# A written-out program with skewed half scans for a convolution, attention and state-space block

## The reference, cut to what matters

```python
x = x + L0(_gn(x))     # group norm, then linear attention with a depthwise 5x5 convolution
x = x + L1(_gn(x))     # group norm, layer norm, then a selective scan (Mamba)

# inside L0: q, k = elu + 1; key weights by a softmax over tokens; rotary turn; kv = k^T v
res = (q_rope @ kv) * z + depthwise5x5(v)
out = w_proj @ (res * o) + b_proj

# inside L1, for each of 4 channel groups of 32 (64 inner channels, 16 states):
def step(h, inp):
    u_t, d_t, B_t, C_t = inp
    h = exp(d_t[:, :, None] * A) * h + (d_t * u_t)[:, :, None] * B_t[:, None, :]
    y = einsum('nds,ns->nd', h, C_t)
    return h, y
# y * silu(z) -> W_out -> skip -> layer norm -> projection
```

## Time and profile before

| | |
|---|---|
| runs of the kernel before | 363.38, 365.04, 365.83 us; median 365.04 |
| profiled execution | span 364.0 us; its own time is not listed apart, the median lies 1.0 above the span |
| VectorE busy | 272.0 us, 75% |
| TensorE busy (matmul) | 273.2 us, 75% |
| ScalarE busy | 218.2 us, 60% |
| GpSimd busy | 201.7 us, 55% |
| transfers | 61.73 MB, 52.6% of the 16 DMA engines' time |

### The profile page before, as it was taken

One profiled execution on the slowest core, in us unless ns is written; L12 is line 12 of the kernel. 1 busy time (PEld: TensorE's weight loads), 2 busy tenths in 40 slices (PEclk: granted clock), 3 DMA queues, 4 the chain that ended last, 5 costly groups with the idle time before them and its releaser, 6 DMA issues.

```text
span 364.0 us, 5551 instructions
## 1 busy us (share of the span) xinstructions
PE 273.2 (75%) x1882; PEld 130.7 (36%) x1882; DVE 272.0 (75%) x334; ACT 218.2 (60%) x408; POOL 201.7 (55%) x135
## 2 busy tenths in 40 slices
PE   1596894899594866987998669878966776965763
PEld 1264552344232333533453235325522211421321
DVE  1632156999212599787999897979999988999992
ACT  2334777563843798359775985697667637552211
POOL 0030302576250279827875797377758666876760
PEclk9999898569788799898799999988999756585598
DMA  7230409730159907782689177908881792197000
GB/s 254 97 90 14 104 16 339 287 88 24 45 127 273 354 34 192 248 306 80 161 292 333 38 206 251 338 27 236 252 307 43 255 309 102 54 331 251 0 14 14
DMA packets 27075, 61.73 MB, mean 170 GB/s; under 512 B 2992, under 2 KB 14896, under 8 KB 27056
## 3 DMA queue, kind: packets, MB, share of 16 engines
q1 hardware_dynamic: 26768, 60.88, 52.6%
q10 hardware_dynamic: 288, 0.61, 0.5%
HBM read 54.62 MB, written 6.86 MB: 169 GB/s over the span
## 4 chain that ended last, share of the span: by engine, by line
PE 30%; DVE 20%; DMA 16%; POOL 9%; issue 9%; ACT 9%; SPq 6%; POOLq 0%; DVEq 0%; ACTq 0%
DVE hst L1190 7%; PE F L430 6%; POOL hst L958 6%; DMA V<-v_scratch 6%; PE DB L554 3%; DVE DB L1165 3%; DMA bc_scratch<-bc 3%; PE Y L581 3%; DVE hst L1177 3%; DVE DB L1161 3%; DMA Cs<-bc_scratch 2%; SPq L253 2%; PE F L408 2%; DVE hst L1180 2%; SPq L229 2%
## 5 line engine op out<-in xcount | busy, mean ns | idle before, releaser
L958 POOL TENSOR_TENSOR hst<-hst,Cs 128x1024 f32<-128x1024 f32 x48 | 113.3, 2361 | 87.9 <-DVE hst L1190 87.9
L1190 DVE TENSOR_TENSOR_SCAN hst<-dec,DB 128x1024 f32<-128x1024 f32 x48 | 109.6, 2283 | 4.4 <-ACT dec L841 3.4
L841 ACT ACTIVATE dec<-dlt,negA 128x1020 f32<-128x1020 f32 x60 | 67.6, 1142 | 17.8 <-DVE hst L1180 9.8
L1165 DVE TENSOR_TENSOR DB<-DB,Bs 128x1024 f32<-128x1024 f32 x48 | 59.0, 1228 | 10.9 <-PE DB L554 5.7
L581 PE MATMUL Y<-hst,CCs 128*32 128x256 f32 x512 | 52.0, 453 | 10.8 <-POOL hst L955 7.0
L955 POOL TENSOR_TENSOR hst<-hst,Cs 128x512 f32<-128x512 f32 x31 | 38.7, 1269 | 15.8 <-DVE hst L1177 15.7
L430 PE MATMUL F<-V,wpatch 128*32 128x256 f32 x512 | 34.8, 395 | 5.0 <-DMA V<-v_scratch 5.0
L581 PEld LDWEIGHTS Y<-hst,CCs 128*32 128x32 f32 x512 | 15.0, 120 | 48.1 <-issue 25.7
L554 PE MATMUL DB<-du,CCs 32*128 32x512 f32 x64 | 24.7, 855 | 4.7 <-DVE DB L1161 4.0
L909 POOL TENSOR_TENSOR tq<-QK,W0s 128x512 f32<-128x512 f32 x8 | 9.0, 1124 | 34.4 <-DVE QK L1071 34.4
L430 PEld LDWEIGHTS F<-V,wpatch 128*32 128x32 f32 x512 | 14.8, 110 | 20.5 <-DMA V<-v_scratch 6.7
(11 more groups left out here) (175 smaller groups left out, 507.9 us busy)
## 6 DMA issues: line engine op xcount, KB each, us to landing
Bs<-bc_scratch SPq DMA_DIRECT2D x32, 512.0 KB, 6.0
Cs<-bc_scratch SPq DMA_DIRECT2D x32, 512.0 KB, 6.9
dlt<-delta_scratch SPq DMA_DIRECT2D x15, 512.0 KB, 5.9
V<-v_scratch SPq DMA_DIRECT2D x32, 200.0 KB, 3.9
XN<-xn_scratch SPq DMA_DIRECT2D x28, 128.0 KB, 3.4
delta_scratch<-delta SPq DMA_DIRECT2D x16, 128.0 KB, 4.2
v_scratch<-vpad SPq DMA_DIRECT2D x8, 211.5 KB, 2.1
bc_scratch<-bc SPq DMA_DIRECT2D x8, 128.0 KB
```

What stands on the lines that cost most here:

```text
L841: af(dec[g % 4][:, :, 1:T], dlt[2 * j + g // SG][:, :, 1:T], ACT.Exp, scale=negA[:, g:g + 1]).then_inc(S("decay_ready"), 1)
L958: tt(hst[g % 4][:], hst[g % 4][:], Cs[g % SG][:], ALU.mult).then_inc(S("hc_ready"), 1)
L1165: v.tensor_tensor(flat(BIN), flat(DU), Bs[g % SG][:], ALU.mult).then_inc(S("b_ready"), 1)
L1190: v.tensor_tensor_scan(hst[g % 4][:], flat(dec[g % 4][:]), flat(BIN), 0.0, ALU.mult, ALU.add).then_inc(S("h_ready"), 1)
```

## The change

1. The loop and the pattern are gone. `program` writes out all eight batches; `places` gives every step of every batch on every engine. All units run in one sequence, so steps of any batch can stand between them.
2. `HALVED = 8`: C-products and collections are made in halves in all batches. VectorE's order is skewed: product half 0 of unit u, scan half 1 of unit u - 1, scan half 0 of unit u, product half 1 of unit u. The broadcast of du is signalled by half.
3. In batch 0, v is projected first into F1, o into DB, and neither stands between k and the scores any more. The first B rows (`Bs[0]`) are broadcast by TensorE from `bc` with a new constant `pickb` and copied by ScalarE; that load is left out. z is copied, and its activation is made with batch 1's, in the same table. `zs` has three buffers.
4. B loads wait for the product of the unit that frees the buffer and not for its C-product; B and C loads have places of their own. For batches 3, 5 and 7 the reload of v stands ahead of the spill of delta that it stood behind; for 4 and 6 it still stands behind it.
5. Convolution steps are four of 32 matmuls and no longer eight of 16.

The core of the diff:

```diff
-        def periods(eng, chains, places, start, unit, finish):
...
+        def program(chains, places, unit, finish):
+
+            works = [begin(chain, b, steps) for chain in chains for b, steps in places[chain.__name__].items()]
+            segment(works, START - 1)
+            for b in range(B):
                 for g in range(GROUPS):
...
+                    seg = iter(range(START + SIDES * (GROUPS * b + g), START + SIDES * (GROUPS * b + g + 1)))
+                    unit(b, b % 2, g, lambda: segment(works, next(seg)))
             finish()
...
+            segment(works, IDLE - 2)
...
-        HALVED = 2
...
+        HALVED = 8
...
+            def bin_half(b, g, half):
+
                 u = GROUPS * b + g
...
+                dve.wait_ge(S(f"du_bc_{half}"), 2 * b + g // SG + 1)
+                if u == 0:
+                    dve.wait_ge(S("b0_ready"), half + 1)
+                elif g < SG:
+                    dve.wait_ge(S(f"b_copied_{g}"), 16 * (b + (g > 0)))
+                wait(dve, ("h_half", "h_ready")[half], u)
+                v.tensor_tensor(BIN[:, half, :], DU[:, half, :], halves(Bs[g % SG], half), ALU.mult).then_inc(
+                    S(("b_half", "b_ready")[half]), 1)
+
+            def scan_half(u, half):
+
+                dve.wait_ge(S(("b_half", "b_ready")[half]), u + 1)
+                dve.wait_ge(S("decay_ready"), u + 1)
+                wait(dve, "y_summed", u - 3)
+                v.tensor_tensor_scan(halves(hst[u % 4], half), flat(dec[u % 4][:, 2 * half:2 * half + 2, :]),
+                                     BIN[:, half, :], 0.0, ALU.mult, ALU.add).then_inc(
+                                         S(("h_half", "h_ready")[half]), 1)
+
+            def unit(b, j, g, side):
+                u = GROUPS * b + g
+                bin_half(b, g, 0)
                 side()
...
+                if u > 0:
+                    scan_half(u - 1, 1)
                 side()
...
+                scan_half(u, 0)
                 side()
+                bin_half(b, g, 1)
                 side()
...
+                pe.wait_ge(S("bc_ready"), b + 1)
+                for half in range(2):
+                    rows = slice(2 * DS * half, 2 * DS * half + 2 * DS)
+                    last = mm(BIN[:, half, :], wt("pickb")[rows], bc[rows, :], start=True, stop=True)
+                last.then_inc(S("b0_done"), 1)
...
+                act.wait_ge(S("b0_done"), 1)
+                for half in range(2):
+                    nc.scalar.copy(halves(Bs[0], half), BIN[:, half, :]).then_inc(S("b0_ready"), 1)
```

Of TensorE's `places`, the steps that stand near the units of batches 0 and 1 (unit u's collection stands between 102 + 4u and just above it):

```diff
+                "lepe": {
...
+                    2: (25.5, 26, 26.5, 27.5,),
+                    3: (114.4, 118.2, 130.01, 130.03,),
+                    4: (142.2, 162, 162.02, 162.04,),
...
+                "mid": {
...
+                    1: (19.5, 20.5, 21.5, 23, 24,),
+                    2: (28, 102.1, 102.3, 114, 114.2,),
...
+                    4: (162.05, 162.07, 162.1, 178, 178.4,),
...
+                "feed": {
+                    0: (20, 22.5, 30, 102,),
+                    1: (118.1, 118.4, 130.07, 134.2,),
+                    2: (146.1, 150.1, 162.09, 166.1,),
...
+                "tail": {
...
+                    1: (28.5, 29.5, 30.5, 102.2,),
...
+                    3: (154, 162.01, 162.03, 162.08,),
```

And of ScalarE's (unit u's decay stands there between 102 + 4u and just above it; in `lead` the fourth step is the copy of `Bs[0]`, in `mid` the sixth writes XN):

```diff
+                "mid": {
...
+                    1: (106.3, 106.5, 106.6, 106.8, 110.2, 110.4,),
...
+                "lead": {
+                    0: (15.5, 16, 16.5, 106.1, 106.4,),
+                },
+                "tail": {
+                    1: (122.03, 122.04, 122.07, 138,),
```

More of the change, by code:

```diff
@@ L134, in advance, with begin @@
         def advance(work):
-            step = next(work[0], IDLE)
-            work[1] = step if work[2] is None else next(work[2], IDLE)
-        def begin(chain, b, j, places=None):
-            work = [chain(b, j), 0, None if places is None else iter(places)]
+            next(work[0], None)
+            work[1] = next(work[2], IDLE)
+        def begin(chain, b, places):
+            work = [chain(b, b % 2), 0, iter(places)]
             advance(work)
@@ L315, in weights @@
-            def weights(b, j):
-                yield from ()
-            places = {
-                "tail": {
-                    1: (102.938, 110.562, 123,),
+            def unit(b, j, g, side):
+                for _ in range(SIDES):
+                    side()
+            places = {
+                "front": {
+                    0: (0, 0.5,),
+                    1: (1, 1.5,),
+                    2: (3.5, 5,),
+                    3: (9, 9.5,),
+                    4: (16.5, 18.5,),
+                    5: (25, 25.5,),
+                    6: (33, 34.5,),
+                    7: (42, 43,),
@@ L335, in _ @@
                 },
             }
-            periods(sp, (weights, front, lepe, mid, tail, back, lead), places, lambda: None, unit, lambda: None)
+            program((front, mid, tail, lead, loads, back), places, unit, lambda: None)
             sp.wait_ge(S("stored"), 16 * B)
@@ L516, in lead, with feed @@
                 last.then_inc(S("delta_bc"), 1)
+            def feed(b, j):
+                for kg in range(2):
+                    for half in range(2):
+                        yield
+                        pe.wait_ge(S("du_ready"), b + 1)
+                        wait(pe, ("b_half", "b_ready")[half], GROUPS * b + SG * kg)
+                        if b == 0 and kg == 0:
+                            pe.wait_ge(S("xs_ready"), 1)
+                        p0 = DI * half + DD * kg
+                        mm(DU[:, half, :], wt("pick")[p0:p0 + DD], du[j][p0:p0 + DD, :], start=True,
+                           stop=True).then_inc(S(f"du_bc_{half}"), 1)
             def skip(b, j):
@@ L546, in back, with unit @@
                 done.then_inc(S("proj2_done"), 1)
-            def broadcast_du(b, j, kg):
-                pe.wait_ge(S("du_ready"), b + 1)
-                wait(pe, "b_ready", GROUPS * b + SG * kg)
-                for half in range(2):
-                    p0 = DI * half + DD * kg
-                    last = mm(DU[:, half, :], wt("pick")[p0:p0 + DD], du[j][p0:p0 + DD, :], start=True, stop=True)
-                last.then_inc(S("du_bc"), 1)
-            def collect(b, j, g):
+            def unit(b, j, g, side):
+                side()
+                side()
                 u = GROUPS * b + g
-                pe.wait_ge(S("hc_ready"), u + 1 if not halved(b) else u)
-                if isinstance(b, int) and b == 0 and g == 0:
+                if not halved(b):
+                    pe.wait_ge(S("hc_ready"), u + 1)
+                if u == 0:
                     pe.wait_ge(S("decay_ready"), SG)
@@ L637, in _ @@
                 },
             }
-            periods(pe, (weights, front, lepe, mid, tail, back, lead), places, start, unit, finish)
+            program((weights, front, lepe, mid, tail, lead, feed, back), places, unit, lambda: None)
         @block.scalar
@@ L1216, in _ @@
                 },
             }
-            periods(dve, (weights, front, lepe, mid, tail, back, lead), places, lambda: None, unit, lambda: None)
+            program((weights, front, mid, tail, lead, back), places, unit, finish)
 def kernel(**inputs):
```

767 lines of the change are left out of this document (396 added, 371 removed), and 39 rows, old and new, of the table places.

## The result

| | before | after |
|---|---|---|
| runs beside each other, median | 365.04 us (361.35 to 367.67) | 351.16 us (344.69 to 354.8) |
| profiled execution: span, granted clock | 364.0 us, 0.861 | 342.9 us, 0.912 |

The ratio is 0.952, with an interval of 0.941 to 0.964. The ratio by itself gives 347.6. Measured once more beside the experiments, the changed kernel took 348.64 us (347.24 to 350.88), ratio 0.963 (0.958 to 0.969). The forecast was 328 with a range of 317 to 345: the direction is right, the gain is 13 to 18 us where 37 were forecast.

What follows compares the result with a forecast made beforehand. VectorE's scans bound seven stretches, latency the one between batches 0 and 1. Sum: 57.1 + 38.9 to unit 8 + 215.3 steady + 8.8 tail + 7 waits = 327 profiled, 328 predicted, range 317 to 345.

Steps and rivals of the forecast that it cites:

- the hole: Latency stretch between batches 0 and 1, VectorE busy 8.38 of 34.47 us; batch 1's second unit at 100, 24 us gained.
- Part 1: Half units and skew on VectorE: 3.42 us a unit instead of 3.59, 2 to 3 us gained in all.
- The new B0 path gains almost nothing: Unit 0's B rows broadcast by TensorE and ScalarE, not memory: unit 0 at 57.1 against 57.95.
- Side work, 23.8: VectorE's steps besides the units in the steady batches, by start-to-start increments: 23.8 us.
- 7 us of residual waits: Steady batches: TensorE's and ScalarE's queued work charged 1 us a batch, 7 us; bounds 0 and 17.
- (a): Rival: no new waits in the steady batches, 321 us; chance 0.15.
- (b): Rival: start hole closes by half, unit 8 at 106, 17 us of waits stay or not: 338 to 345; chance 0.12.
- (c): Rival: VectorE's half units are paid by duration, not by start: 343 us; chance 0.05.
- (d): Rival: TensorE's clumps cost 2.4 us at each of 15 places: 350, or 340 with half of them; chance 0.12.
- (e): Rival: slower than before, TensorE's clumps at over 3.0 us each in 15 places: 370 us; chance 0.04.
- (f): Rival: ScalarE's decays and not the scans pace the kernel: 365 us; chance 0.02.
- Part 2: Start of batch 0: v projected first, new path for first B rows; counted queue times put unit 0 at 57.1.

Runs made afterwards that it cites:

- e2: Changed kernel without the memory trips of v (batches 1 to 7) and of the normalized input (batches 2 to 7), C loads kept: 334.85 us, ratio 0.915.
- d2: Changed kernel with half the convolution matmuls in batches 1 to 7, without both trips and without C loads after batch 0: 337.84 us, ratio 0.921.
- d1: Changed kernel with half of the convolution's matmuls left out in batches 1 to 7, all trips kept: 356.07 us, ratio 0.973.
- e1: Changed kernel with half of the convolution's matmuls issued twice in batches 1 to 7: 354.02 us, ratio 0.971.
- b4: Changed kernel without the skew, each second half scan right behind its own product: 371.34 us, ratio 1.017.
- b2: Changed kernel with unit 40's du broadcasts and batch 4's x projection moved in TensorE's order, and four loads moved on SP: 348.04 us, ratio 0.958.
- d4: Changed kernel with the C loads of batches 1 to 7 issued from ScalarE's queue: 364.11 us, ratio 0.997.
- b1: Changed kernel with unit 40's du broadcasts and batch 4's x projection moved in TensorE's order: 349.17 us, ratio 0.964.
- c1: Changed kernel with whole, unskewed products, scans, C-products and collections in batches 0 to 5: 388.13 us, ratio 1.057.

## Why the prediction was right or wrong

- **What bounds, and the hole: right.** Unit 0 at 56.24 (57.1 forecast), unit 4's first scan held to 81.36 (81), unit 8 at 98.23 (96), unit 9 at 102.99 (100). The chain walked through the queues held to 3 us, and the hole gave 21.3 us of 24.
- **Half units, 3.42 apart: right.** Two units without side steps between them: 133.97 to 137.39.
- **"A gain of about 0.4 each, 2 to 3 us in all": not shown in the steady batches, wrong as the price of Part 1.** The starts are as counted, but unit 9 to the last scan takes 231.2 us after 231.0. Skew and halves together keep this order from costing 34 to 39 us, and 14 to 18 with its broadcasts in pairs. The prediction priced the form by VectorE alone and not by what it asks of TensorE.
- **"The new B0 path gains almost nothing": right at unit 0, wrong for the time.** It is worth 6 to 9 us against the load in its old place, by the queue that it leaves.
- **Side work, 23.8: 3.7 us too small.** 236.0 us from unit 8, less 17.0 of waits (all 18.0, without the 1.0 at unit 8 itself), is 219.0 where 215.3 were forecast.
- **"7 us of residual waits": the step that failed.** 17.0 came. The prediction charged TensorE's clumps 1 us a batch and took the V reload as loosened by its new place or as having slack; the input's trip it charged only in the start. But the longest wait stands at batch 7, whose reload does go ahead of delta's spill (224.33). What the runs showed in its place: late trips of v and of the input, worth 14 to 17 us together (e2); with them gone the waits are 9.0 us. The clumps' length carries nothing once the trips are gone (d2); what it carries beside them is open (d1, e1).
- **Rivals.** (a) needed no waits. (b)'s number, 338 to 345 with 17 us of waits, is near, but not its reason: the hole did close. (c) fell: the Trainium skill, page "VectorE: DVE Perf Modes", section on the TRN2 errata, lets many small tiles pay what one large pays once, and the durations do (1.21 a half scan), but the starts overlap as long as no instruction needs the one just ahead; where it does (b4), 0.26 us a unit come back. (d), clumps that cost 2.4 us at 15 places, came at three places (1.8, 2.5 and 4.8 us), the two longer ones behind a trip. (e) and (f) fell.
- **The sum of the miss.** Profiled: 0.9 earlier at unit 0, 3.1 later from there to unit 8, 3.7 side work, 10.0 waits, 0.1 less tail: 15.8, from 327.1 to 342.9. The rest to the median of 351.16 is scatter: this kernel's runs spread over 10 us and the one profiled was the fastest. The 1.0 us from span to time was a small slip as well: each execution takes 1.8 us more than its own span (344.69 and 342.9).
- **Two readings of the old rows.** The waits from 112 to 294 have two more between the 5.7 and the 2.8 us: 3.9 for a collection and 3.4 for a decay, single ones, both in the hole, so the sum of 17 does not change. And the description's 128 convolution matmuls are 64 in the trace; the queue times of Part 2 count them as the trace does.

Of the trips' 14 to 17 us two forms were not told apart: the transfers' own time beside loads of 512 KB, and SP's standing until a write has landed. By the profiles both are there: V's copies at unit 40 are used 9.5 us after the first issue, the slowest 7.9 us from its own issue to landing, and in the second order experiment (b2) SP stood from 163.4 to 170.0 for the input's write, with five loads behind it:

```profile
163.07 0.34 SPq L208 DMA_DIRECT2D xn_scratch<-XN  x1
170.05 1.73 SPq L213 DMA_DIRECT2D XN<-xn_scratch  x4
```

The Trainium skill, page "DMA: Bandwidth & Descriptors", section "Two DMAs through the same engine are not ordered", says that a load which reads what an earlier one wrote needs the completion semaphore in between; no run here leaves that wait out. By that rule the standing can be moved to another queue but not left out. Moving C loads to ScalarE (d4) was the only such move tried.

## What to carry to other kernels

Treat the queue through which a write and read back go in order as a resource of its own: list, for each unit, every chain that passes through it, since here removing the wait that the profile names only showed the next one (b1), while leaving the trips out halved the waits (e2). Price a form (halves, skew) by what it lets the other engines do late, not only by its engine's own starts. A transfer taken out of a crowded queue is worth what stands behind it, even if the point that it served does not move.

## What was unexpected of the hardware

With 224 recorded matmuls less TensorE was busy as long as before, 270.9 against 271.4 us, at a granted clock of 0.862 against 0.913, a mean over the two levels of 1.2 and 2.4 GHz. The Trainium skill, page "TensorE: Matmul & The Clock Gate", section "What's actually happening", says that activity is what releases the throttle; the half convolution agrees, the one with 224 more, at 0.895, does not. In whole units (c1) TensorE stood 4.02 us before 166.97, and then two matmuls of the B and C rows took 1.97 us at 168.98, at a granted clock of 0.50 although TensorE was busy without a gap from 168.9 to 181. The changed kernel's second measurement, with 1.19 us of standing in that place and a clock of 1.00, has 1.07 us for the same two. TensorE was slow just where VectorE waited for it.
